# Four graph layers in one Trainium2 kernel: products and copies of the first layer and of the borders between layers reordered, and the third layer's bias rows written by ScalarE

## The chip, the core and the metric

The kernel runs on one core of one Trainium2 chip. The core has five engines with a program each: TensorE (PE in the rows, its weight loads PEld), VectorE (DVE), ScalarE (ACT), GpSimd (POOL) and SyncE (SP), which here only issues DMAs. The engines wait for each other by semaphores, and each works through its own list in the order in which it is written. The metric is the device time of one execution in microseconds (us); lower is better. The kernel before took 1655.96 us in the median of 3 runs (1653.0 to 1656.04).

## What is computed

Four message-passing layers follow one another over a graph of 50000 nodes with 128 features and 12500 edges sorted by target. Each is added to its input and normalized over the features:

```python
x = _layernorm(x + _L0_gnn_ref(x, edge_index, edge_weight, edge_attr_64, L0_gnn_Wq, ...))
x = _layernorm(x + _L1_gnn_ref(x, src, dst, L1_gnn_W1, L1_gnn_b1, L1_gnn_W2, L1_gnn_b2))
x = _layernorm(x + _L2_gnn_ref(x, L2_gnn_weight, src, dst, edge_type_8))
x = _layernorm(x + _L3_gnn_ref(x, L3_gnn_W_e, L3_gnn_b_e, L3_gnn_W_n, L3_gnn_b_n, src, dst,
                               edge_type_3, node_type_3))
```

The first layer is attention over the edges of a target (softmax by segments, plus `bias`), the second takes the mean of the sources and two linear maps with biases, the third multiplies each source by one of 8 matrices and sums, the fourth has 3 edge types and 3 node types: for a node of type t the result is `agg @ W_n[t].T + b_n[t]`, where `agg` begins with `relu(node_feature)`.

## The kernel before

Most nodes are the target of no edge, so for them a layer is the same dense map on all rows. The kernel therefore computes two things side by side: a dense pass over all 50000 rows, in NC = 100 blocks of 500 rows (4 tiles of 125 partitions), and the exact rows of the edges, in EC = 25 chunks of 500 edges. The dense results are written first, and in the last layer the rows of nodes with edges are scattered over them.

A dense block d goes through three stations. Its first-layer rows (`y0`, then normalized to `x1`) are made in step d; LAG = 3 blocks later the second layer (`y1` to `x3`), and 3 blocks later again the fourth (`sel` to `res`). One set of four PSUM banks, `po`, serves all of this: in each bank 3 × 128 columns hold the fourth layer's results for the three node types, and the last 128 the second layer's product z. So one round of TensorE is: `turn_rt` (transpose `x3`, ScalarE copies it to `rt` with a relu), `turn_xt` (transpose `x1`, ScalarE copies it to `xt`), then `dense_products`: `biased_slots` writes the bias rows `b_n` into the 3 × 128 columns of all four banks by a bf16 product (`po<-ball,ones_bf`), `types` adds `rt` times `wnt` on top, and `z_products` writes `xt` times `wab`. VectorE's `read(d)` then takes z out (L796), picks among the three types (L799, L800) and forms `sel` (L802). It increments `s_read`, which frees the banks for the next round. `measure` and `variances` give the variances of the new rows, ScalarE takes ln and exp of them (`first_roots`, "seed" in the rows), and VectorE's `scales` makes `rst` and `nmr` (L778 to L781) and increments `s_ln`; after it ScalarE normalizes (`third_rows`, `first_rows`, `results_of`, all L1074).

The order is written out by hand on every engine, as a loop over chunks c with one or two dense blocks in each step:

- First layer (lines "layer0"): two blocks per step. TensorE's step c has `back0(c)`, block 2c, the second half with block 2c+1, and between them the scores of chunk c+2, which end with `turn_targets0` (transpose of the gathered targets), ScalarE's copy `dt` and `score_targets` (L1500). ScalarE's slopes (L1151), differences and exponentials and VectorE's scans turn them into weights.
- Second layer: one block per step.
- Third layer: one block per step. VectorE makes masks for 7 relations (`masks`, L969), TensorE multiplies them with 8 matrices (`relations2`, L1627), VectorE scans the result by segments (`run<-same,run,pb`), TensorE transposes the scan (`pa<-ident,run`, L1645), and `target_rows2` adds it.
- Fourth layer: no dense block is left but the last few at the border.

Between the layers stand a few steps with dense blocks alone (`only_dense`), while the edge rows of the layer that ended are stored to HBM and gathered again by GpSimd for the next. GpSimd's gathers of node types (`types2`, 100 of them, needed at the start of the fourth layer) fill its free time.

## Time and profile before

| what | value |
|---|---|
| median of 3 runs | 1655.96 us |
| the profiled execution | 1652.15 us, of which the span of the trace is 1650.4 us |
| mean granted TensorE clock | 0.929 |
| busy share of the span | PE 84%, DVE 86%, ACT 67%, POOL 75% |
| first layer | 0 to about 590 us |
| second layer | about 612 to 889 us |
| third layer | about 933 to 1247 us |
| fourth layer | from about 1290 us |

The shares of the whole span mix stages with different limits, so the stretches have to be read by themselves. In a row of a timeline the first number is the start in us, the second how long the group lasted, and the note in brackets is the idle time before it with what ended it. "Granted clock" is the share of TensorE's full clock: 1.00 is 2.4 GHz and 0.50 is 1.2 GHz.

### The profile page before, as it was taken

The page shows a single profiled execution, that of the slowest core. Times are in us where ns is not written, and L with a number is a line of the kernel's source. Part 1 is how long each engine was busy: PE and PEld are TensorE (multiplying, and loading weights), DVE is VectorE, ACT ScalarE, POOL GpSimd, SP SyncE. Part 2 cuts the span into 40 slices and gives each one's busy share as a digit, 9 for nine tenths or more (in the row PEclk, how much of TensorE's full clock was granted, in tenths as well). Part 3 has the DMA queues.
Part 4 walks back from the last instruction along what each step waited for, and adds up shares of the span by engine and source line. Part 5 has one row for each costly group of instructions (what it writes and reads, how often), then busy time and mean ns, then how long its engine had stood idle before and what let it go on. Part 6 is the DMA issues. An engine that isn't in the chain of part 4 may idle for free.

```text
span 1650.4 us, 22899 instructions
## 1 busy us (share of the span) xinstructions
PE 1388.8 (84%) x6078; PEld 890.6 (54%) x6078; DVE 1419.0 (86%) x3056; ACT 1110.9 (67%) x2769; POOL 1230.3 (75%) x910
## 2 busy tenths in 40 slices
PE   3788877788778868777776899999996899999995
PEld 2455554555545546666665555555553455555552
DVE  5899899999899879999998799999995677777773
ACT  1678788887788787888888577777774344444441
POOL 7888888877777857888874567777778488888873
PEclk9798888988889879999998999999998899999997
DMA  7344444434444256767675455556554344344320
GB/s 172 94 100 102 111 109 110 112 91 115 111 113 105 58 139 177 189 179 192 182 187 149 131 149 164 156 157 165 151 133 111 83 97 96 96 97 97 96 70 20
DMA packets 165797, 205.06 MB, mean 124 GB/s; under 512 B 66825, under 2 KB 97920, under 8 KB 165668
## 3 DMA queue, kind: packets, MB, share of 16 engines
q1 hardware_dynamic: 108068, 179.45, 40.0%
q0 software_dynamic: 57600, 24.15, 9.0%
q8 instruction: 50, 0.82, 0.2%
q14 instruction: 79, 0.65, 0.2%
HBM read 147.12 MB, written 70.80 MB: 132 GB/s over the span
## 4 chain that ended last, share of the span: by engine, by line
PE 44%; DVE 32%; ACT 12%; issue 10%; POOL 1%; DMA 1%; SPq 0%; DVEq 0%; POOLq 0%; ACTq 0%
PE po L1391 23%; DVE bst L756 8%; DVE masked L969 6%; PE pt L1380 5%; PE pc L1500 3%; PE po L1386 3%; ACT x L1074 3%; DVE run L831 2%; PE po L1451 2%; DVE y L796 2%; DVE po L799 2%; DVE sel L802 2%; DVE po L800 2%; ACT do L1074 2%; PE pa L1672 1%
## 5 line engine op out<-in xcount | busy, mean ns | idle before, releaser
L536 POOL DMA_INDIRECT xs<-target_rows,slot_all x236 | 322.2, 1365 | 140.9 <-issue 60.9
L1074 ACT ACTIVATE x<-y,nmr,rst 125x128 f32<-125x128 f32 x800 | 322.5, 483 | 29.6 <-issue 18.4
L1391 PE MATMUL po<-wnt,rt 128*125 128x384 f32 x800 | 297.4, 518 | 0.0
L1380 PE MATMUL pt<-ident,x 125*128 125x125 f32 x800 | 122.3, 276 | 110.5 <-issue 110.5
L1391 PEld LDWEIGHTS po<-wnt,rt 128*125 128x125 f32 x800 | 162.7, 206 | 96.9 <-issue 21.2
L1391 PE MATMUL po<-wnt,run 128*125 128x384 f32 x600 | 201.5, 486 | 0.0
L543 POOL DMA_INDIRECT out_rows<-do,last_all x100 | 146.5, 1465 | 63.0 <-issue 40.6
L1380 PEld LDWEIGHTS pt<-ident,x 125*128 125x128 f32 x800 | 93.1, 145 | 148.4 <-issue 147.1
L536 POOL DMA_INDIRECT xs<-in_x,src_all x100 | 143.2, 1432 | 34.7 <-issue 33.8
L1074 ACT ACTIVATE do<-yd,nmr,rst 125x128 f32<-125x128 f32 x400 | 163.5, 483 | 5.4 <-DVE nmr L781 4.6
L1074 ACT ACTIVATE res<-sel,nmr,rst 125x128 f32<-125x128 f32 x400 | 163.7, 484 | 2.6 <-DVE nmr L781 1.8
L1627 PE MATMUL pb<-masked,wr 128*128 128x500 f32 x350 | 156.5, 588 | 2.2 <-DVE masked L969 2.2
L536 POOL DMA_INDIRECT slot_all<-slot_d,src_all x100 | 131.9, 1319 | 30.5 <-issue 30.5
L536 POOL DMA_INDIRECT ntd_all<-in_ntype,dst_all x100 | 129.4, 1294 | 30.5 <-issue 30.5
L543 POOL DMA_INDIRECT slot_d<-eid,last_all x100 | 128.5, 1285 | 30.5 <-issue 30.2
L756 DVE BATCH_NORM_STATS2 bst<-y 125x6 f32<-125x256 f32 x400 | 143.1, 420 | 3.8
L1391 PEld LDWEIGHTS po<-wnt,run 128*125 128x125 f32 x600 | 108.9, 188 | 68.7 <-issue 0.6
L1140 ACT ACTIVATE st<-pt 128x500 f32<-128x500 f32 x50 | 29.3, 585 | 142.1 <-issue 95.1
L536 POOL DMA_INDIRECT xdb<-target_rows,slot_all x64 | 86.6, 1352 | 44.2 <-issue 29.3
L536 POOL DMA_INDIRECT xd<-in_x,dst_all x68 | 94.9, 1396 | 27.2 <-issue 19.2
L1386 PE MATMUL po<-ball,ones_bf 128*125 128x384 bf16 x412 | 102.2, 379 | 13.0 <-DVE sel L802 13.0
L1451 PEld LDWEIGHTS po<-wab,xt 128*125 128x125 f32 x800 | 101.5, 188 | 19.8
(190 smaller groups left out, 3035.1 us busy)
## 6 DMA issues: line engine op xcount, KB each, us to landing
xin<-in_x SPq DMA_DIRECT2D x100, 224.0 KB
out_rows<-res SPq DMA_DIRECT2D x100, 224.0 KB
source_rows<-so SPq DMA_DIRECT2D x75, 224.0 KB
target_rows<-do SPq DMA_DIRECT2D x75, 224.0 KB
xs<-source_rows SPq DMA_DIRECT2D x59, 224.0 KB
same<-same_d SPq DMA_DIRECT2D x50, 250.0 KB
rel<-in_etype SPq DMA_DIRECT2D x50, 250.0 KB
xd<-target_rows SPq DMA_DIRECT2D x46, 224.0 KB
```

Of the source, the lines that this page charges most:

```text
L536: return nc.gpsimd.indirect_dma_start(out=to, out_offset=None, in_=table, in_offset=bass.IndirectOffsetOnAxis(ap=index, axis=0), bounds_ch ...
L543: return nc.gpsimd.indirect_dma_start(out=table, out_offset=bass.IndirectOffsetOnAxis(ap=index, axis=0), in_=of, in_offset=None, bounds_ch ...
L756: last = V.bn_stats(to, y[:, j:j + 2, :].rearrange("p j d -> p d j"))
L796: last = V.scalar_tensor_tensor(out=y1[(d - LAG) % 4][:, :, :], in0=of_z, scalar=0.0, in1=x1[(d - LAG) % 4][:, :, :], op0=ALU.max, op1=ALU ...
L969: V.scalar_tensor_tensor(out=masked[:, r, :], in0=rel[b][:, :], scalar=float(r), in1=st[:, :], op0=ALU.is_equal, op1=ALU.mult).then_inc(q[ ...
L1074: last = A(to[:, j, :], y[:, j, :], ACT.Identity, scale=rst[s][:, k:k + 1], bias=nmr[s][:, k:k + 1])
L1380: last = nc.tensor.transpose(tile_of(to, j), rows_[:, j, :], ident[0:R, 0:R])
L1386: mm(po[0:R, j * 512:j * 512 + NT * D], ones_bf[:, 0:R], ball[:, :, :].rearrange("k s d -> k (s d)"), start=True, stop=False, skip_group_c ...
L1391: last = mm(po[0:R, j * 512:j * 512 + NT * D], left(j), wnt[:, k, :, :].rearrange("k t d -> k (t d)"), start=start, stop=stop, skip_group_ ...
L1451: last = mm(po[0:R, j * 512 + NT * D:(j + 1) * 512], xt[:, j, :], wab[:, 0, :], start=False, stop=True, skip_group_check=True)
L1500: mm(pc[:, 0:C], qs[:, :], dt[:, :], start=False, stop=True).then_inc(q["pA"], 1)
L1627: mm(pb[:, 0:C], wr[:, r, :], masked[:, r, :] if r else st[:, :], start=r == 0, stop=r == REL - 1).then_inc(q["pM"], 1)
```

## The change

In the third layer, ScalarE writes a whole row `bfull` (the three bias rows and 128 zeros) into each of the four banks `po` by one ACTIVATE of 125 × 2048, `biased_slots2`. TensorE's bf16 product is gone there, and its `types` waits for `fB` in place of `s_read`. In the first layer TensorE multiplies block 2c+1's `types` ahead of the transposed targets and the scores, and ScalarE takes the roots ahead of the copy `dt`. At the borders, some copies, roots and gathers are put in another place, and 15 of GpSimd's type gathers move from the third layer into the last five steps of the second.

```diff
+        bfull = sb("bfull", [R, NT + 1, D])
...
 (GpSimd, second layer)
+                if SOONER * T + 3 * c >= EC * T:
+                    types2(typed, typed + 3)
+                    typed += 3
             types2(typed, typed + 2 * T)
...
 (VectorE, set-up)
+            V.memset(bfull[:, NT, :], 0.0)
+            V.tensor_copy(bfull[:, 0:NT, :], brow[0:R, :, :])
...
 (ScalarE, first layer)
             for c in range(EC):
                 s = chain_of(2 * c) % 2
                 first_roots(s, 8)
+                if c >= 1 and there(c + 1):
+                    evacuate_targets(c + 1, 0, 0, dt, ACT.Copy)
                 if there(c + 1):
                     slopes0(c + 1)
...
                     target_rows0(c, TAIL, 0)
+                    evacuate_rt(2 * EC - 2)
                     source_rows0(c, s)
+                    evacuate_xt(2 * EC - 2)
+                    first_roots(chain_of(2 * EC) % 2, 4)
                     results_of(2 * c, s, 2)
                     results_of(2 * c + 1, s, 3)
-                if there(c + 2):
-                    evacuate_targets(c + 2, 0, 0, dt, ACT.Copy)
-            only_dense(2 * EC)
+            chain_rows(2 * EC)
...
 (ScalarE, third layer)
+            def biased_slots2(c):
+
+                act.wait_ge(s_read, block_of(2, c) + 1)
+                A(po[0:R, :].rearrange("p (j k) -> p j k", j=T), bfull[:, :, :].rearrange("p s d -> p (s d)").unsqueeze(1).broadcast_to([R, T, 512]),
+                  ACT.Copy).then_inc(ph[2]["fB"], 1)
...
                 act.wait_ge(s_ln, k + 1)
                 third_rows(d, k % 2, 0)
+                biased_slots2(c)
                 evacuate_rt(d - 1)
                 first_rows(d, k % 2, 2)
...
 (ScalarE, start of the fourth layer)
             targets3(0)
+            evacuate_sources(1, 3, 0)
             dense_chain(NC + 2 * LAG - 1)
-            evacuate_sources(1, 3, 0)
...
 (TensorE, first layer)
                     turn_xt(2 * c + 1)
+                    if 2 * c + 1 >= LAG:
+                        type_products(2 * c + 1)
+                    else:
+                        pe.wait_ge(s_read, 2 * c + 4)
+                        biased_slots()
                     if there(c + 2):
                         turn_targets0(c + 2)
+                    z_products(2 * c + 1).then_inc(s_z, 1)
+                    if there(c + 2):
                         score_targets(c + 2)
-                    dense_products(2 * c + 1)
...
 (TensorE, start of the third layer)
             dense_turns(d - 2)
-            dense_products(d - 2)
             pe.wait_ge(ph[1]["rd"], EC)
             turns2(0)
+            dense_products(d - 2)
...
 (TensorE, third layer)
                 if there(c + 1):
                     relations2(c + 1, range(REL // 2, REL))
-                dense_products(d - 2)
+                    pe.wait_ge(q["fB"], c + 1)
+                    pe.wait_ge(s_rt, d - 4)
+                    last = types(lambda j: rt[:, j, :], 0, stop=False)
+                    if d - 2 < NC:
+                        last = z_products(d - 2)
+                    last.then_inc(s_z, 1)
+                else:
+                    dense_products(d - 2)
```

The semaphore `s_fill` is also folded into `s_const`, whose waits count one higher.

On ScalarE one step of the third layer runs from the roots (`seed`) to the next roots. `x_1<-y_1` are the third rows, `rt` and `xt` the copies of the two transposes, `st` the copy of the sources. Before:

```order
L1083 ACTIVATE seed<-seed 125x16 [waits s_logs]
L1074 ACTIVATE x_1<-y_1,nmr,rst 125x128 [waits s_ln]
L1074 ACTIVATE x_1<-y_1,nmr,rst 125x128 x3
L1111 ACTIVATE rt<-pt 128x500 [waits s_tr]
L1074 ACTIVATE x_0<-y_0,nmr,rst 125x128 x4
```

Now:

```order
L1089 ACTIVATE seed<-seed 125x16 [waits s_logs]
L1080 ACTIVATE x_1<-y_1,nmr,rst 125x128 [waits s_ln]
L1080 ACTIVATE x_1<-y_1,nmr,rst 125x128 x3
L1288 ACTIVATE po<-bfull 125x2048 [waits s_read]
L1117 ACTIVATE rt<-pt 128x500 [waits s_tr]
L1080 ACTIVATE x_0<-y_0,nmr,rst 125x128 x4
```

The fill of the four banks stands behind the rows that wait for `s_ln`, and ahead of the copy `rt`.

On TensorE the end of one step of the third layer and the start of the next, from the last relations. Before:

```order
L1627 MATMUL pb<-masked,wr 128x500 [waits layer2_vM] x3
L1386 MATMUL po<-ball,ones_bf 125x384 [waits s_read]
L1386 MATMUL po<-ball,ones_bf 125x384 x3
L1391 MATMUL po<-wnt,rt 125x384 [waits s_rt]
L1391 MATMUL po<-wnt,rt 125x384 x3
L1451 MATMUL po<-wab,xt 125x128 [waits s_xt]
L1451 MATMUL po<-wab,xt 125x128 x3
L1645 MATMUL pa<-ident,run 125x128 [waits s_ln,layer2_vA]
L1645 MATMUL pa<-ident,run 125x128 x3
L1380 MATMUL pt<-ident,x_0 128x125 [waits s_xt,s_x3]
```

Now:

```order
L1653 MATMUL pb<-masked,wr 128x500 [waits layer2_vM] x3
L1411 MATMUL po<-wnt,rt 125x384 [waits s_rt,layer2_fB]
L1411 MATMUL po<-wnt,rt 125x384 x3
L1471 MATMUL po<-wab,xt 125x128 [waits s_xt]
L1471 MATMUL po<-wab,xt 125x128 x3
L1671 MATMUL pa<-ident,run 125x128 [waits s_ln,layer2_vA]
L1671 MATMUL pa<-ident,run 125x128 x3
L1400 MATMUL pt<-ident,x_3 128x125 [waits s_xt,s_x3]
```

The bias product is gone; the product with `rt` waits for `fB`, and everything of the next step stands behind it.

On TensorE the second half of a step of the first layer, from the transpose of `x1` of block 2c+1 to the first row of the next step (`xdb` are the gathered targets). Before:

```order
L1380 MATMUL pt<-ident,x_3 128x125 [waits s_xt,s_rt,s_x1]
L1380 MATMUL pt<-ident,x_3 128x125 x3
L1380 MATMUL pt<-ident,xdb 128x125 [waits s_xt,layer0_eS,layer0_gd_2]
L1380 MATMUL pt<-ident,xdb 128x125 x3
L1500 MATMUL pc<-dt,qs 128x500 [waits layer0_eD]
L1386 MATMUL po<-ball,ones_bf 125x384 [waits s_read]
L1386 MATMUL po<-ball,ones_bf 125x384 x3
L1391 MATMUL po<-wnt,rt 125x384 [waits s_rt]
L1391 MATMUL po<-wnt,rt 125x384 x3
L1451 MATMUL po<-wab,xt 125x128 [waits s_xt]
L1451 MATMUL po<-wab,xt 125x128 x3
L1514 MATMUL pb<-ident,run 125x128 [waits layer0_vL,layer0_nF,layer0_vA]
```

Now:

```order
L1400 MATMUL pt<-ident,x_3 128x125 [waits s_xt,s_rt,s_x1]
L1400 MATMUL pt<-ident,x_3 128x125 x3
L1406 MATMUL po<-ball,ones_bf 125x384 [waits s_read]
L1406 MATMUL po<-ball,ones_bf 125x384 x3
L1411 MATMUL po<-wnt,rt 125x384 [waits s_rt]
L1411 MATMUL po<-wnt,rt 125x384 x3
L1400 MATMUL pt<-ident,xdb 128x125 [waits s_xt,layer0_eS,layer0_gd_2]
L1400 MATMUL pt<-ident,xdb 128x125 x3
L1471 MATMUL po<-wab,xt 125x128 [waits s_xt]
L1471 MATMUL po<-wab,xt 125x128 x3
L1520 MATMUL pc<-dt,qs 128x500 [waits layer0_eD]
L1534 MATMUL pb<-ident,run 125x128 [waits layer0_vL,layer0_nF,layer0_vA]
```

The score product moved from ahead of the block's products to behind them.

## Rows read from the trace of the kernel before

**Rows 1.** Busy time by stage: stretch, its length, each engine's busy time, clock, DMA.

```profile
0.00:590.00 590.00, 460.53 (x2028) 296.87 (x2028) 516.32 (x1085) 440.80 (x1112) 469.29 (x350) 0.86 0.46 109
933.00:1247.00 314.00, 306.67 (x1242) 183.82 (x1240) 304.58 (x663) 228.44 (x587) 226.22 (x170) 1.00 0.57 151
```

**Rows 2.** VectorE's scans by layer: duration min/median/max ns, first and last start.

```profile
L831 DVE TENSOR_TENSOR_SCAN run<-masked,run,aux x25: 1259/1260/1262, 31.0 to 564.2; 128x500 f32<-128x500 f32 x25
L831 DVE TENSOR_TENSOR_SCAN run<-same,run,pb x25: 1244/1257/1257, 933.3 to 1246.2; 128x500 f32<-128x500 f32 x25
```

**Rows 3.** Timeline of one step of the third layer.

```profile
1013.19 0.70 PE L1645 MATMUL pa<-ident,run 128*125 128x128 f32 x4 [0.31 <-DVE run L831]
...
1014.36 0.59 ACT L1111 ACTIVATE rt<-pt 128x500 f32<-128x500 f32 x1 [0.73 <-issue]
...
1016.58 0.68 DVE L796 SCALAR_TENSOR_TENSOR y<-po,x 125x512 f32<-125x512 f32 x1
...
1018.63 0.69 DVE L802 SCALAR_TENSOR_TENSOR sel<-x,po 125x512 f32<-125x512 f32 x1
...
1021.73 0.81 PE L1386 MATMUL po<-ball,ones_bf 128*125 128x384 bf16 x4
...
1022.38 2.74 PE L1391 MATMUL po<-wnt,rt 128*125 128x384 f32 x8
...
1024.01 0.22 ACT L1083 ACTIVATE seed<-seed 125x16 f32<-125x16 f32 x1
...
1024.88 0.18 DVE L781 SCALAR_TENSOR_TENSOR nmr<-bst,rst 125x16 f32<-125x16 f32 x1
...
1024.96 1.04 PE L1451 MATMUL po<-wab,xt 128*125 128x128 f32 x8
...
1025.10 1.65 ACT L1074 ACTIVATE x<-y,nmr,rst 125x128 f32<-125x128 f32 x4 [0.87 <-DVE nmr L781]
...
1026.31 0.70 PE L1645 MATMUL pa<-ident,run 128*125 128x128 f32 x4 [0.31 <-DVE run L831]
```

**Rows 4.** ScalarE's copies without pointer operands: count, busy us, mean ns.

```profile
L1140 ACT ACTIVATE st<-pt 128x500 f32<-128x500 f32 x50 | 29.3, 585 | 142.1 <-issue 95.1 <-PE pt L1380 47.1
...
L1169 ACT ACTIVATE den<-pc 125x12 f32<-125x12 f32 x25 | 4.5, 180 | 37.3 <-PE pa L1518 31.8 <-issue 5.5
```

**Rows 5.** TensorE by microsecond at the third layer's end: busy, granted clock, DMA.

```profile
1251.00:1252.00 1.00, 0.00 (x0) 1.00 0.62 125
...
1253.00:1254.00 1.00, 0.00 (x1) 0.50 0.05 1
...
1259.00:1260.00 1.00, 1.00 (x6) 0.99 0.76 96
```

**Rows 6.** Timeline of the same stretch, TensorE.

```profile
1254.00 1.54 PE L1386 MATMUL po<-ball,ones_bf 128*125 128x384 bf16 x4 [5.38 <-DVE sel L802]
1255.33 4.57 PE L1391 MATMUL po<-wnt,rt 128*125 128x384 f32 x8
```

**Rows 7.** Timeline of one step of the first layer, its second half.

```profile
233.69 0.62 PE L1380 MATMUL pt<-ident,x 125*128 125x125 f32 x4 [2.06 <-issue]
...
237.49 2.04 PE L1500 MATMUL pc<-dt,qs 128*128 128x500 f32 x2 [0.68 <-ACT dt L1145]
...
237.84 0.19 DVE L778 SCALAR_TENSOR_TENSOR tmp<-seed 125x32 f32<-125x32 f32 x1 [1.08 <-ACT seed L1083]
...
239.56 0.59 ACT L1151 ACTIVATE masked<-pc 128x500 f32<-128x500 f32 x1 [1.75 <-PE pc L1500]
```

**Rows 8.** Timelines at the three borders.

```profile
599.40 1.06 PE L1380 MATMUL pt<-ident,x 125*128 125x125 f32 x4 [11.45 <-issue]
...
919.75 0.17 DVE L778 SCALAR_TENSOR_TENSOR tmp<-seed 125x16 f32<-125x16 f32 x1 [8.70 <-ACT seed L1083]
...
1262.04 1.27 POOL L536 DMA_INDIRECT xdb<-target_rows,slot_all  x1 [0.30 <-issue]
...
1285.89 2.03 PE L1672 MATMUL pa<-st,wet 128*128 128x500 f32 x2 [7.40 <-ACT st L1140]
```

More of the change, by code:

```diff
@@ L158, in gnn_kernel @@
             sem, ("s_w0", "s_w1", "s_w2", "s_w3", "s_same", "s_idx", "s_slotrow", "s_prep", "s_scr", "s_pe0", "s_bp", "s_const"))
[L159 to L160 removed]
+        s_rdeg, s_rd, s_hs, s_last, s_turned, s_carry, s_before = map(
+            sem, ("s_rdeg", "s_rd", "s_hs", "s_last", "s_turned", "s_carry", "s_before"))
         s_xin, s_res = [sem(f"s_xin{i}") for i in range(4)], two(sem, "s_res")
@@ L277, in _ @@
             sp.dma_start(nt_all[:, :, :], ntypeP).then_inc(s_last, 16)
-            sp.wait_ge(s_fill, 1)
+            sp.wait_ge(s_const, 2)
             sp.dma_start(slot_d.rearrange("(p t) o -> p (t o)", p=R), fill[:, :]).then_inc(s_slotrow, 16)
@@ L527, in _ @@
             nc.gpsimd.memset(prv[:, :], -1).then_inc(s_const, 1)
-            nc.gpsimd.memset(fill[:, :], SKIP).then_inc(s_fill, 1)
+            nc.gpsimd.memset(fill[:, :], SKIP).then_inc(s_const, 1)
             nc.gpsimd.iota(row_id[:, :], pattern=[[1, PM]], base=0, channel_multiplier=PM)
@@ L570, in types2 @@
                     gather(ntd_all[:, i // T, i % T:i % T + 1], ntype3, dst_all[:, i // T, i % T:i % T + 1], N - 1).then_inc(s_types, 16)
-            pool.wait_ge(s_const, 2)
+            pool.wait_ge(s_const, 3)
             pool.wait_ge(s_idx, 80)
@@ L684, in _ @@
             step = chain.step
-            dve.wait_ge(s_const, 2)
+            dve.wait_ge(s_const, 3)
             dve.wait_ge(s_idx, 80)
@@ L1124, in dense_chain, with chain_rows @@
             def dense_chain(d):
+                first_roots(chain_of(d) % 2, 4)
+                chain_rows(d)
+            def chain_rows(d):
                 k = chain_of(d)
-                first_roots(k % 2, 4)
                 act.wait_ge(s_ln, k + 1)
@@ L1415, in setup_carry @@
                 mm(pb[0:1, D:D + R], rdeg_p[:, PM - 1:PM], ident[0:R, 0:R], start=True, stop=True).then_inc(s_carry, 1)
-                pe.wait_ge(s_const, 2)
+                pe.wait_ge(s_const, 3)
                 pe.wait_ge(s_turned, 2)
```

4 lines of the change are left out of this document (1 added, 3 removed).

## The prediction

> **What bounds the kernel now.** I read the busy times by stage first, then the periods of each loop, then the timeline of one step of each stage that the change touches, and the borders last. In the third layer two engines are full: VectorE is busy 304.58 us of 314 and TensorE 306.67, at the full clock (2.4 GHz), while ScalarE has 228.44 [rows 1]. Its 25 scans start from 933.3 to 1246.2 [rows 2], and in the step shown the period is 1026.31 - 1013.19 = 13.12 us [rows 3]. VectorE sets it: L796 and `sel` have no wait noted, and TensorE's only idle time in the step is the 0.31 us before `pa<-ident,run`, which waits for VectorE's scan. L796 starts at 1016.58, though the z products before it, the twins of those at 1024.96, had been done for over 3 us. So TensorE's bias product, 1022.38 - 1021.73 = 0.65 us a step, hides behind VectorE, and removing it alone would give nothing there.
>
> In the first layer no engine is full (VectorE 516.32 us of 590, TensorE 460.53, ScalarE 440.80) and the clock is 0.86 [rows 1]. The loop takes (564.2 - 31.0)/24 = 22.2 us a step on average [rows 2] and goes round by handoffs: copy of a transpose, next transpose, copy `dt`, score, slopes [rows 7].
>
> **Third layer: where the fill lands.** In step c TensorE's `types` wants ScalarE's fill number c+1. By the order on ScalarE that fill stands behind the third rows, which wait for `s_ln` of the same step c. Take the step of [rows 3]. VectorE frees the banks when `sel` ends, at 1019.3; TensorE reaches `types` at 1021.73. But the last of VectorE's scales (L781) starts at 1024.88, and the third rows, which wait for it, at 1025.10. They take 1.65 us, so the fill starts at 1026.75. The banks have been free for 7.4 us by then, and TensorE has stood for 5. The wait for `s_read` costs nothing; it is the place behind `s_ln` that costs.
>
> Behind the waiting `types` on TensorE are the z products, the transposes of the scan, and `turn_rt`. VectorE's L796 waits for z, and ScalarE's copy `rt`, which stands right behind the fill, waits for `turn_rt`. So the fill closes a ring that was open before, in which each link waits for the one ahead:
>
> - fill on ScalarE. No row shows ScalarE writing PSUM. From 180 ns at 12 columns and 585 ns at 500 [rows 4] a column costs 0.83 ns, and 2048 columns make 180 + 2036 × 0.83 = 1870 ns. Below, 1.2 us, if a write to PSUM were a third cheaper than one to SBUF; above 3.7 us, if it were twice as dear. I take 1.87, as the rows are copies of the same kind. (The Trainium skill's page "ScalarE: Activation LUTs", section "Step-by-step: what each stage is for", calls PSUM the quicker port of the two for a ScalarE result; no run here shows it, and by it the fill would be nearer the lower end.)
> - weights, `types` and z on TensorE. From 1022.38 to 1024.96 and 1.04 more is 3.62 us; with the first weight load (some 0.15) and the handoff (0.05) 3.82 us at full clock.
> - from the first `pa<-ident,run` to the third rows of the next step: 1025.10 - 1013.19 = 11.91 us [rows 3]. ScalarE has its whole list here (`rt`, first rows, `st`, `xt`, source rows, target rows, results, roots), and it waits for TensorE at `rt` already in the row (0.73 us), so the stretch begins with that handoff and can't shrink much.
> - third rows: 1.65 us.
>
> Sum: 1.87 + 3.82 + 11.91 + 1.65 = 19.25 us a step, against 13.12.
>
> The clock comes on top. TensorE works some 12.5 us in such a step (13.12 less its wait of 0.31 and the bias product), so it is idle for 6.7 us in each. In [rows 6] it has been idle for 5.38 us before 1254.00; in [rows 5] the granted clock is 1.00 at 1251, 0.50 (1.2 GHz) at 1253 and back at 1259. The eight products there start at 1255.33, behind the bias product at 1254.00, and last 4.57 us against 2.74 at full clock [rows 3], 1.83 more. Without a bias product ahead of them they meet the slow stretch from its start, and at half clock throughout they would take 2.58 us more. I take 2.1. That makes 21.35 us a step, 8.2 more than before.
>
> The Trainium skill has a rule on this: its page "TensorE: Matmul & The Clock Gate", section "HAM oscillation — how this bites in real kernels", says that a loop with a long enough idle stretch in every round is throttled in every round again, so that the cost is paid each time. The trace agrees at this one place, with its 0.50 at 1253 [rows 5]; without the rule's repetition the sum stays at 19.25 us a step.
>
> 24 steps (c = 0 to 23) have a fill. 24 × 8.2 = 197, less 2 for the first one, where only VectorE's leg is late: **+195 us**.
>
> **First layer.** TensorE now does the bias product and `types` of block 2c+1 (0.65 + 2.58 at full clock) between the transpose that ends at 234.31 and the turning of the targets, which is on the path to the score. The transposes are then done at 238.1 (0.6), `dt` at 238.8 (0.6, as the copies of [rows 4]) and the score, half of 2.04 at full clock, at 240.2, the z products standing before it. ScalarE's slopes start at 240.3 and not at 239.56 [rows 7]: 0.7 us later. In return, at the step's start TensorE has no products of block 2c+1 left to do, and ScalarE no longer waits at `den`: that wait is 31.8 us in 25 steps, 1.3 each [rows 4]. Taking the roots first removes VectorE's 1.08 us at L778 [rows 7]; but its next wait is then for the slopes, so this only moves. Net 0.6 a step in 24 steps, **-15 us**. Bounds: if VectorE's 1.08 counted as well, -40; if `types`, now on the path, ran at half clock, 2.6 us a step more, +45.
>
> **Borders.** First to second: TensorE's 11.45 us without work before 599.40 [rows 8] shrink, as the copies `rt` and `xt` and the roots go ahead of the results (8 activations, 3.2 us): -3, no more, since the second layer also needs its first gathers. Second to third: VectorE's 8.70 us at 919.75 end 5 us earlier, because `turns2(0)` no longer waits for a block's products; GpSimd's 15 type gathers come before its first gathers of the third layer and delay them a little, into that gap: -5. Third to fourth: the first gathers of the fourth layer, at 1262.04, stood behind 17 type gathers, of which 2 are left, and start when the last target rows have landed, some 3 us sooner; `st` of chunk 1 is copied before the last dense chain, which cuts the 7.40 us before 1285.89 by some 2 on the path: -5. Together **-13**, with bounds from 0 to -22.
>
> Filling `bfull` is a copy of 384 columns and a small memset on VectorE at the start, and the changed count of `s_const` orders nothing anew: 0, or 1 us if no wait covers them.
>
> **Sum.** 1652.15 + 195 - 15 - 13 = **1819 us**. The profiled execution lies 0.2% below the median of the runs, so this may come out some 4 us higher.
>
> **The rivals.**
> 1. The ring closes, but the clock stays up: 24 × 6.13 - 2 - 28 = +117, **1769 us**. Transposes and relations fill 12.5 us of each step; against it stands [rows 5].
> 2. Only VectorE's leg of the ring is closed. If ScalarE found slack in its list, the step would be third rows 1.65, fill 1.87, products 3.82 and then VectorE from L796 to the end of its scales, 1025.06 - 1016.58 = 8.48: 15.8 us, with the clock's 2.1 17.9. 24 × 4.8 - 28 = +87, **1739 us**. Against it: ScalarE's list is in order, and its 9.5 us of work a step (228.44/24) start only behind `rt`.
> 3. The other side: the fill is hidden. If ScalarE could write the banks in the gap from 1019.3 to 1021.7, TensorE would never wait, VectorE would go on setting 13.12 us, and only the 28 us of reorderings would be left: **1624 us**. It decides at whether the fill of step c is ahead of TensorE's `types` of step c; the order puts it 5 us behind.
> 4. The clock falls in the first layer too, with `types` on the path: 24 × 2.6 = +62, **1881 us**. Before, it fell there after two gaps close together; now the 2.06 us before 233.69 [rows 7] are followed by unbroken work.
>
> **How the numbers follow.** Forecast (ring with clock) 0.68, rival 1 0.15, rival 2 0.07, rival 3 0.04, rival 4 0.06. The range runs from just below rival 1, 1758, to a fill twice as dear, 1819 + 24 × 1.85 = 1863. A measurement of this kernel can tell some 0.2% from no change. Faster has rival 3 and a little more, 0.05; nothing lands within 0.2% but by chance, 0.01; slower 0.94.
>
> **What would show it.** In the profile after: `po<-wnt,rt` in the third layer has a wait of 6 to 7 us ended by ScalarE's `po<-bfull`, 24 times; the scans there are 21 us apart (19 if the clock holds); VectorE waits for z ahead of `y<-po,x` and for the seeds ahead of its scales; the fill lasts 1.9 us; the granted clock of the stretch is 0.8 to 0.85; the fourth layer is as long as before. In the first layer `den` waits less, the slopes' wait is longer and the one before L778 is gone. The prediction is wrong if the scans of the third layer stay 13.1 us apart.

## The result and the profile after

| | median | range | ratio to the kernel before (95%) |
|---|---|---|---|
| before | 1655.14 us | 1653.0 to 1656.04 | |
| changed | 1832.69 us | 1830.92 to 1835.58 | 1.1084 [1.1071, 1.1098] |

The changed kernel is 10.8% slower (four runs of each). Left out of all medians and ratios are three much longer executions, one of the last experiment's kernel (1948.29 us) and two of the repeated kernel before (1757.99 and 6931.33 us). The changed kernel's profiled execution took 1830.92 us with a span of 1829.1 us, 178.7 us more than the 1650.4 us of before. The mean granted clock fell from 0.929 to 0.890.

I divided the span at VectorE's scans, which both kernels have in the same number. They start so in the changed kernel (line, engine, operation, count, shortest/median/longest ns, first and last start in us):

```profile
L837 DVE TENSOR_TENSOR_SCAN run<-masked,run x50: 1247/1256/1261, 38.5 to 605.7; 128x500 f32<-128x500 f32 x50
L837 DVE TENSOR_TENSOR_SCAN run<-same,run,st x25: 1251/1255/1262, 633.1 to 909.5; 128x500 f32<-128x500 f32 x25
L837 DVE TENSOR_TENSOR_SCAN run<-same,run,pb x25: 1250/1256/1258, 953.5 to 1433.6; 128x500 f32<-128x500 f32 x25
```

| stretch, between scans | before | changed | difference |
|---|---|---|---|
| to the first layer's last scan | 584.7 | 605.7 | +21.0 |
| border to the second layer | 28.1 | 27.4 | -0.7 |
| second layer | 274.5 | 276.4 | +1.9 |
| border to the third layer | 46.0 | 44.0 | -2.0 |
| third layer | 312.9 | 480.1 | **+167.2** |
| border to the fourth layer | 31.7 | 30.7 | -1.0 |
| first two steps of the fourth layer | 28.8 | 21.1 | -7.7 |
| the rest of it | 302.5 | 302.5 | 0 |

From the last scan to the end both kernels take about 41.2 us, and the differences add up to the 178.7 us. The third layer has nearly all of it. The +1.9 us of the second layer lie in its first interval alone (12.37 us where it was 10.45), so the first border and what follows from it cost 1.2 us and give nothing. Busy time by stage, in the columns of [rows 1]:

```profile
0.00:611.00 611.00, 457.39 (x2028) 297.62 (x2028) 515.60 (x1086) 442.30 (x1111) 465.65 (x350) 0.85 0.44 105
953.00:1434.00 481.00, 326.92 (x1139) 184.67 (x1137) 309.03 (x664) 269.12 (x610) 222.33 (x165) 0.84 0.37 98
```

VectorE has the same work there as before (309.03 us against 304.58) but 481 us to do it in, and TensorE's clock fell from 1.00 to 0.84. No engine is full any more: this is a stage that waits. The waits of the third layer say for whom (engine, tile and line, the one waited for, then us in all, times, longest):

```profile
PE po L1411 <- ACT po L1288: 153.4, 23, 6.7
ACT rt L1117 <- PE pt L1400: 145.4, 23, 6.3
DVE y L802 <- PE po L1471: 98.0, 23, 4.8
DVE masked L975 <- PE pb L1653: 45.4, 22, 2.7
```

TensorE waits for ScalarE's fill, ScalarE for a transpose of TensorE, VectorE for TensorE's z: each waits for another once a step. One turn of this, where before stood [rows 3]:

```profile
1212.18 0.17 DVE L787 SCALAR_TENSOR_TENSOR nmr<-bst,rst 125x16 f32<-125x16 f32 x1
...
1212.39 1.65 ACT L1080 ACTIVATE x<-y,nmr,rst 125x128 f32<-125x128 f32 x4 [0.91 <-DVE nmr L787]
...
1213.95 1.86 ACT L1288 ACTIVATE po<-bfull 125x2048 f32<-125x2048 f32 x1
...
1215.86 4.47 PE L1411 MATMUL po<-wnt,rt 128*125 128x384 f32 x8 [6.70 <-ACT po L1288]
...
1220.16 1.04 PE L1471 MATMUL po<-wab,xt 128*125 128x128 f32 x8
...
1221.04 0.60 PE L1671 MATMUL pa<-ident,run 128*125 128x128 f32 x4
1221.24 0.69 DVE L802 SCALAR_TENSOR_TENSOR y<-po,x 125x512 f32<-125x512 f32 x1 [4.16 <-PE po L1471]
...
1222.10 0.59 ACT L1117 ACTIVATE rt<-pt 128x500 f32<-128x500 f32 x1 [6.30 <-PE pt L1400]
...
1232.85 1.65 ACT L1080 ACTIVATE x<-y,nmr,rst 125x128 f32<-125x128 f32 x4 [0.88 <-DVE nmr L787]
```

From one third rows to the next are 1232.85 - 1212.39 = 20.46 us; between the sixth scan of the layer and the twenty-first the mean is 20.48. The granted clock in this turn (TensorE by microsecond, as [rows 5]):

```profile
1211.00:1212.00 1.00, 0.00 (x0) 1.00 0.87 254
1213.00:1214.00 1.00, 0.00 (x0) 0.50 0.79 205
1218.00:1219.00 1.00, 1.00 (x3) 0.50 0.62 125
1220.00:1221.00 1.00, 1.00 (x10) 1.00 0.12 2
```

It falls to 1.2 GHz while TensorE stands idle in front of the fill, is low through most of `types`, and is back at 2.4 GHz for z.

In the first layer, one step with the slow stretch behind the score (compare [rows 7]):

```profile
243.32 0.56 ACT L1117 ACTIVATE rt<-pt 128x500 f32<-128x500 f32 x1
...
250.08 0.59 ACT L1161 ACTIVATE masked<-pc 128x500 f32<-128x500 f32 x1 [1.20 <-PE pc L1520]
...
251.58 0.67 PE L1534 MATMUL pb<-ident,run 128*125 128x128 f32 x4 [1.54 <-DVE masked L848]
...
255.18 0.16 ACT L1179 ACTIVATE den<-pc 125x12 f32<-125x12 f32 x1
...
255.54 2.00 PE L1526 MATMUL pa<-st,wv 128*128 128x500 f32 x2 [1.86 <-ACT den L1180]
...
258.17 1.88 PE L1509 MATMUL pc<-ea,es 65*128 65x500 f32 x2
...
260.56 0.59 ACT L1150 ACTIVATE st<-pt 128x500 f32<-128x500 f32 x1 [0.55 <-PE pt L1400]
```

Ahead of the score the step is now as planned (it takes 1.07 us and not 2.04). But TensorE has nothing to do behind it, 1.54 and then 1.86 us, since the block that used to stand there now stands ahead. The same places before:

```profile
233.02 0.57 ACT L1111 ACTIVATE rt<-pt 128x500 f32<-128x500 f32 x1
...
246.08 0.18 ACT L1169 ACTIVATE den<-pc 125x12 f32<-125x12 f32 x1 [1.32 <-PE pa L1518]
...
246.47 1.08 PE L1506 MATMUL pa<-st,wv 128*128 128x500 f32 x2
...
247.81 1.01 PE L1489 MATMUL pc<-ea,es 65*128 65x500 f32 x2
...
249.55 0.58 ACT L1140 ACTIVATE st<-pt 128x500 f32<-128x500 f32 x1
```

The granted clock in the changed kernel is 0.50 from 254 to 260:

```profile
252.00:253.00 1.00, 1.00 (x12) 1.00 0.29 65
254.00:255.00 1.00, 0.00 (x0) 0.50 0.14 10
259.00:260.00 1.00, 1.00 (x3) 0.50 0.64 163
```

At the borders, the gathers of the fourth layer start 1450.29 - 1433.6 = 16.7 us behind the last scan, where it was 15.9 us, and the wait for `st` of 7.40 us [rows 8] is 0.68:

```profile
1450.29 1.27 POOL L537 DMA_INDIRECT xdb<-target_rows,slot_all  x1 [45.25 <-DMA target_rows<-do]
...
1465.57 1.11 PE L1705 MATMUL pa<-st,wet 128*128 128x500 f32 x2 [0.68 <-ACT st L1150]
```

### The profile page after: what moved, and what is told of

Its sections match the earlier page's. It is cut to its first block, busy times and chain, and to the rows that moved or that the text cites. A ratio compares the mean times of both kernels' runs of the same rounds, so it can differ in the third digit from the quotient of the medians.

```text
span 1829.1 us, 22757 instructions
## 1 busy us (share of the span) xinstructions
PE 1406.3 (77%) x5982; PEld 894.0 (49%) x5982; DVE 1423.2 (78%) x3058; ACT 1154.7 (63%) x2793; POOL 1230.3 (67%) x910
## 4 chain that ended last, share of the span: by engine, by line
PE 54%; ACT 20%; DVE 17%; issue 7%; POOL 1%; DMA 1%; SPq 0%; ACTq 0%; POOLq 0%; DVEq 0%
PE po L1411 27%; ACT x L1080 6%; PE pt L1400 6%; DVE bst L762 5%; PE pb L1653 4%; ACT res L1080 4%; PE po L1471 3%; PE pa L1526 3%; ACT po L1288 2%; ACT do L1080 2%; PE po L1406 2%; DVE run L837 2%; PE pc L1509 2%; ACT so L1295 2%; PE pc L1520 1%
## 5 line engine op out<-in xcount | busy, mean ns | idle before, releaser
L537 POOL DMA_INDIRECT xs<-target_rows,slot_all x236 | 326.8, 1385 | 263.5 <-DMA xs<-source_rows 180.4
L1411 PE MATMUL po<-wnt,rt 128*125 128x384 f32 x800 | 325.2, 557 | 156.6 <-ACT po L1288 156.6
L1080 ACT ACTIVATE x<-y,nmr,rst 125x128 f32<-125x128 f32 x800 | 322.3, 481 | 28.8 <-DVE nmr L787 28.8
L1411 PEld LDWEIGHTS po<-wnt,rt 128*125 128x125 f32 x800 | 170.6, 219 | 284.2 <-ACT po L1288 176.0
L1400 PE MATMUL pt<-ident,x 125*128 125x125 f32 x800 | 137.4, 300 | 105.3 <-issue 105.3
L1400 PEld LDWEIGHTS pt<-ident,x 125*128 125x128 f32 x800 | 103.4, 157 | 156.7 <-issue 156.6
L802 DVE SCALAR_TENSOR_TENSOR y<-po,x 125x512 f32<-125x512 f32 x100 | 68.7, 687 | 138.1 <-PE po L1471 138.1
L544 POOL DMA_INDIRECT slot_d<-eid,last_all x100 | 137.6, 1376 | 30.5 <-issue 30.5
L537 POOL DMA_INDIRECT xs<-in_x,src_all x100 | 133.5, 1335 | 34.9 <-issue 34.6
L1117 ACT ACTIVATE rt<-pt 128x500 f32<-128x500 f32 x100 | 57.3, 573 | 156.1 <-PE pt L1400 156.1
L975 DVE SCALAR_TENSOR_TENSOR masked<-rel,st 128x500 f32<-128x500 int32 x175 | 107.0, 671 | 45.4 <-PE pb L1653 45.4
```

What stands on the lines that cost most here:

```text
L537: return nc.gpsimd.indirect_dma_start(out=to, out_offset=None, in_=table, in_offset=bass.IndirectOffsetOnAxis(ap=index, axis=0), bounds_ch ...
L544: return nc.gpsimd.indirect_dma_start(out=table, out_offset=bass.IndirectOffsetOnAxis(ap=index, axis=0), in_=of, in_offset=None, bounds_ch ...
L802: last = V.scalar_tensor_tensor(out=y1[(d - LAG) % 4][:, :, :], in0=of_z, scalar=0.0, in1=x1[(d - LAG) % 4][:, :, :], op0=ALU.max, op1=ALU ...
L975: V.scalar_tensor_tensor(out=masked[:, r, :], in0=rel[b][:, :], scalar=float(r), in1=st[:, :], op0=ALU.is_equal, op1=ALU.mult).then_inc(q[ ...
L1080: last = A(to[:, j, :], y[:, j, :], ACT.Identity, scale=rst[s][:, k:k + 1], bias=nmr[s][:, k:k + 1])
L1117: A(rt[:, :, :], by_tile(pt), ACT.Relu).then_inc(s_rt, 1)
```

## The experiments

All ratios are to the kernel before, run on the same chip in the same session. "Step" is the mean distance of the third layer's scans 6 to 21, or in the first layer that of its scans `run<-masked,run,aux` from the sixth on. My theory was: the third layer's ring costs some 165 us, the first layer costs 21 where a gain was forecast, the borders give a little.

### The parts by themselves

**The third layer undone.** The changed kernel with the third layer as before:

```diff
                 third_rows(d, k % 2, 0)
-                biased_slots2(c)
                 evacuate_rt(d - 1)
...
-                    pe.wait_ge(q["fB"], c + 1)
-                    pe.wait_ge(s_rt, d - 4)
-                    last = types(lambda j: rt[:, j, :], 0, stop=False)
...
+                dense_products(d - 2)
```

> The changed kernel with the third layer as it was before (TensorE writes the bias rows by its product, no fill on ScalarE). If the stages add up as the two traces show them (third layer +167 us, first layer +21, the rest -9.5), this takes 1655 + 21 - 9.5 = 1667 us. Rival: the reorderings are a gain of 28 us as forecast, and the loss in the first layer only comes with the rest: 1627 us.

Measured: 1657.99 us, 1.0027 [1.0017, 1.0038]. The third layer is back at 312.9 us, the first one stays at 606.9, and the border to the fourth is 24.6 us where the changed kernel has 30.7. So the ring also hides some 6 us of what the edits at that border give. All the other edits together are a small loss and not the gain of 28 us that I forecast. The edits at the borders were not run by themselves.

**The third layer alone.** The kernel before, with nothing but the fill, its order and its wait:

```diff
                 third_rows(d, k % 2, 0)
+                biased_slots2(c)
...
+                    pe.wait_ge(q["fB"], c + 1)
+                    pe.wait_ge(s_rt, d - 4)
+                    last = types(lambda j: rt[:, j, :], 0, stop=False)
```

> The kernel before with the third layer's part of the change alone. Ring theory: its scans are 20.5 us apart, and it takes 1655 + 167 = 1822 us. Rival: part of the loss came from the gathers moved by GpSimd or from the start of the third layer, so that it is under 1800.

Measured: 1820.49 us, 1.1004 [1.0982, 1.1026], steps of 20.49 us, third layer 482.3 us. This part accounts for nearly all of the 10.8%.

**TensorE's order of the first layer alone.** The kernel before, with the block 2c+1 moved:

```diff
+                    if 2 * c + 1 >= LAG:
+                        type_products(2 * c + 1)
...
                     if there(c + 2):
                         turn_targets0(c + 2)
+                    z_products(2 * c + 1).then_inc(s_z, 1)
+                    if there(c + 2):
                         score_targets(c + 2)
-                    dense_products(2 * c + 1)
```

> The kernel before with TensorE's new order in the first layer alone (bias product, types, targets, z, score). If this order causes the first layer's loss by moving the slow stretch of TensorE's clock onto values0 and the transposes, it takes the +21 us and more, since the roots still stand behind the copy of the targets: 1676 to 1690 us. Rival (ScalarE's order causes the loss): 1655 or less.

Measured: 1680.32 us, 1.0166 [1.0148, 1.0184]; the last scan of the layer starts at 610.7 us, 26.0 later than before. The loss in the first layer comes from this order. The steps are 23.89 us, and 23.87 in the changed kernel; the 5 us that this kernel loses beyond the changed one's 21.0 lie in the first five steps.

**Roots first alone.** ScalarE takes the roots ahead of the copy `dt`, and nothing else is changed:

```diff
                 first_roots(s, 8)
+                if c >= 1 and there(c + 1):
+                    evacuate_targets(c + 1, 0, 0, dt, ACT.Copy)
...
-                if there(c + 2):
-                    evacuate_targets(c + 2, 0, 0, dt, ACT.Copy)
```

> The kernel before with ScalarE's new order in the first layer alone (roots ahead of the copy of the targets). VectorE's wait of 1.08 us for the seeds goes; if that was on the path it gains up to 25 us (1630), if it only moves to the next wait it is the same, 1655. Rival: ScalarE is later at the copy by 0.5 us a step, 1667.

Measured: 1652.33 us, 0.9996 [0.9987, 1.0006], steps of 23.03 us as before. VectorE's wait for the seed only moved: from 100 to 550 us it waited 17.3 us there before and 11.6 for z; now it waits 10.8 us behind the slopes (L841) and 17.1 for z.

### Is it the fill's place, its length, or the clock?

**The fill in the gap.** The fill of step c+1 is issued in step c behind `xt` and ahead of the source rows, where the banks have just been read; the work is the same.

```diff
+            biased_slots2(0)
             for c in range(EC - 1):
...
                 third_rows(d, k % 2, 0)
-                biased_slots2(c)
...
                 evacuate_xt(d - 1)
                 if there(c + 2):
+                    biased_slots2(c + 1)
                     source_rows2(c + 2)
```

> The changed kernel, with ScalarE's fill of step c+1 put ahead of the source rows of step c, where VectorE has just freed the banks; the same 24 fills, no wait for the scales in front of them. Ring theory: TensorE no longer waits 6.7 us for it and the clock stays up; but ScalarE's list had no slack ahead of the roots (they start the moment the results end), so 1.9 us of work there lengthens the step to 14.9: 1667 + 24 x 1.8 = 1710 us. Rival (VectorE sets the pace and a fill is hidden anywhere off the ring): 13.1 us a step, 1667 us. Rival (the fill itself, its write into PSUM, is what costs): 20 us a step, 1830.

Measured: 1729.38 us, 1.0459 [1.0441, 1.0478], steps of 16.22 us, not the 14.9 that I expected. More than half of the loss is gone with the place alone. What is left shows in one step (timeline):

```profile
1152.12 1.89 ACT L1288 ACTIVATE po<-bfull 125x2048 f32<-125x2048 f32 x1
...
1154.69 2.74 PE L1412 MATMUL po<-wnt,rt 128*125 128x384 f32 x8
...
1159.02 0.17 DVE L784 SCALAR_TENSOR_TENSOR tmp<-seed 125x16 f32<-125x16 f32 x1 [2.76 <-ACT seed L1089]
...
1161.06 0.70 PE L1672 MATMUL pa<-ident,run 128*125 128x128 f32 x4 [2.75 <-DVE run L837]
```

TensorE doesn't wait for the fill any more, and `types` runs at full clock. But the fill has pushed ScalarE's roots back. VectorE waits 2.76 us for them, its scan is late, TensorE idles 2.75 us for the scan, and the clock falls at the relations that follow:

```profile
1161.00:1162.00 1.00, 0.94 (x8) 1.00 0.78 238
...
1163.00:1164.00 1.00, 1.00 (x2) 0.50 0.73 228
```

The clock is also most of the miss. From the second step on to the last but two, the layer's steps take either 15.1 to 15.2 us, near the 14.9, or 16.6 to 16.7. In all short ones the granted clock is 1.00 throughout, in all long ones its mean is 0.90.

**The fill in the gap and the roots first.** The same, with the results' rows (`results_of`) moved behind the roots of the next step, so that the roots don't wait for the added 1.9 us:

```diff
                 first_roots(k % 2, 4)
+                if c >= 1:
+                    results_of(d - 1, (k - 1) % 2, 1)
...
-                if there(c + 2):
-                    results_of(d, k % 2, 1)
```

> As the kernel with the fill in the gap, but ScalarE takes the roots ahead of the results, so that 1.5 us of rows leave the path to the roots and 1.9 us of fill are on it. Theory (ScalarE's list ahead of the roots sets the step there): 13.5 us a step instead of 16.2, and with so little idle time on TensorE the clock stays at 1.00; 1729 - 24 x 2.7 = 1664 us, at best equal to the third layer as it was before (1658). Rival (the fill itself slows TensorE or VectorE by their sharing of the banks): 15 us a step or more, 1700.

Measured: 1672.4 us, 1.0121 [1.0098, 1.0144], steps of 13.59 us against 13.12, third layer 324.6 us. VectorE's wait for the seed is down to 0.42 us:

```profile
1159.63 0.17 DVE L784 SCALAR_TENSOR_TENSOR tmp<-seed 125x16 f32<-125x16 f32 x1 [0.42 <-ACT seed L1089]
```

The same 24 fills, well placed, cost 11.7 us in the layer and not 167. They gain nothing either, since the bias product that they replace was hidden behind VectorE. The granted clock of the layer is 1.00 here, where it was 0.93 with the roots late.

**A small write in the fill's place.** ScalarE writes one column to a tile of its own where the fill stood, and TensorE makes its bias product itself, ahead of the same wait. What is left is the wait for a place in ScalarE's list:

```diff
+        tick = sb("tick", [R, 1])
...
-                A(po[0:R, :].rearrange("p (j k) -> p j k", j=T), bfull[:, :, :].rearrange("p s d -> p (s d)").unsqueeze(1).broadcast_to([R, T, 512]),
-                  ACT.Copy).then_inc(ph[2]["fB"], 1)
+                A(tick[:, :], none[:, :], ACT.Copy).then_inc(ph[2]["fB"], 1)
...
+                    pe.wait_ge(s_read, d + 1)
+                    for _ in range(1):
+                        biased_slots()
                     pe.wait_ge(q["fB"], c + 1)
```

> The changed kernel with ScalarE's fill replaced by a write of one column to another tile, at the same place in its list and with the same waits; TensorE makes the bias product itself, ahead of its wait for ScalarE. What is left is the wait alone. Ring theory: 1.7 us less in each round than the changed kernel, 20.47 - 1.7 = 18.8 us a step, 1833 - 24 x 1.7 = 1792 us. Rival (the length of the fill is the cost): 13.1 us a step, 1667 us.

Measured: 1801.39 us, 1.0888 [1.0864, 1.0912], steps of 19.41 us. Taking out the fill's 1.86 us of ScalarE's time saves only 1.07 a step, 24 us in the layer of the 167 (480.1 to 456.5). The miss of 0.6 us against the expected step is the clock's: `types` meets more of the slow stretch than in the changed kernel. From its start to the first `pa` are 5.85 us on average over 23 steps, against 5.20 there. It differs from step to step (4.2 to 5.5 us); one of the dear ones:

```profile
1162.77 5.48 PE L1411 MATMUL po<-wnt,rt 128*125 128x384 f32 x8 [4.35 <-issue]
```

**The same, with TensorE kept at work.** The bias product is made nine times over ahead of the wait, eight of them to no use:

```diff
                     pe.wait_ge(s_read, d + 1)
-                    for _ in range(1):
+                    for _ in range(9):
                         biased_slots()
                     pe.wait_ge(q["fB"], c + 1)
```

> As the kernel with the small write, but TensorE makes its bias product 9 times over before the wait (the last one counts), so that it is at work through most of the stretch in which it would stand idle. Ring theory with the clock: the products after the wait run at full clock and the step loses another 1.7 us, 17.1 us a step, some 40 us less than the kernel with the small write (1750 us). Rival (the clock has no part in it, the extra work is only in the way): the same as with the small write or more.

Measured: 1768.29 us, 1.0699 [1.0676, 1.0722], steps of 17.74 us.

```profile
1159.39 6.01 PE L1406 MATMUL po<-ball,ones_bf 128*125 128x384 bf16 x36
...
1164.33 0.19 ACT L1289 ACTIVATE tick<-none 125x1 f32<-125x1 f32 x1
...
1165.24 2.74 PE L1411 MATMUL po<-wnt,rt 128*125 128x384 f32 x8
```

The nine held `types` back until 1165.24, 0.7 us behind the write's end at 1164.52, so this is what the step has over the expected 17.1. The granted clock of the layer is 1.00, and `types` takes 2.74 us in every step. The same wait with TensorE at work costs 1.67 us a step less than with it idle (19.41 - 17.74). From the start of `types` to the first `pa` it is 2.4 us less (3.45 against 5.85), of which the nine take 0.7 back: the 2.4 are the clock's share.

### The first layer: the clock

**Useless products at two places.** The third layer undone (as in the first experiment), and in the first layer from its third step on, four further f32 products of 384 columns a step into the bank of the next transposes, two ahead of `back0` (the transposes of the scan and the products for the denominators) and two behind it; they are overwritten by what comes next:

```diff
+            def keep():
+                mm(pt[:, 0:NT * D], wnt[:, 0, 0, :], wnt[:, 0, :, :].rearrange("k t d -> k (t d)"), start=True, stop=True)
...
+                if c >= 2:
+                    for _ in range(2):
+                        keep()
                 back0(c)
+                if c >= 2 and c < EC - 1:
+                    for _ in range(2):
+                        keep()
```

> The changed kernel with the third layer as before, and two products without use (384 columns, fp32, into the free bank of the transposes) ahead of and two behind back0 in each step of the first layer from the third on, in the gaps after which the clock falls. Theory: the clock stays at 1.00 over values0, the transposes and the features, and the step goes from 23.9 to 22.0 us: 1667 - 22 x 1.9 = 1625 us. Rival (the clock is not the cause of the first layer's loss, or the extra products delay what stands behind them): 1667 us or more.

Measured: 1645.85 us, 0.9963 [0.9948, 0.9978]: a gain of 0.6% on the kernel without them (0.9963 against 1.0027), and not the 2% that I expected. From the fifth step on three take 21.9 us and all others 23.6. In the slow ones another gap, that for the turn of `xt`, lets the clock fall:

```profile
260.85 0.62 PE L1399 MATMUL pt<-ident,x 125*128 125x125 f32 x4 [2.07 <-issue]
...
262.32 2.13 PE L1410 MATMUL po<-wnt,rt 128*125 128x384 f32 x3
```

**At all gaps.** Three more ahead of that transpose, behind a wait for the bank's last reader (`keep` now takes the bank and the count):

```diff
+                    if c >= 2:
+                        pe.wait_ge(ph[0]["nF"], c + 1)
+                        keep(pb, 3)
                     turn_xt(2 * c + 1)
```

> As the kernel with the products without use in the first layer, and three more of them ahead of the transpose of x1 of block 2c+1, into the bank pb, where TensorE still stood idle for 2.07 us. In the trace of that kernel the steps in which the clock stayed up took 21.9 us and the others 23.6. Theory: all steps take 21.9; 1646 - 18 x 1.7 = 1615 us. Rival (the 21.9 us had another cause): 1646 us or more.

Measured: 1617.96 us, 0.9794 [0.9777, 0.9811]. Every step from the fifth on takes 21.9 us, and the layer's last scan starts at 566.6, 40.3 us earlier than in the first experiment, by nothing but useless work.

**The old order, kept busy.** The kernel before with the changed borders alone, and five useless products a step round the transpose of block 2c+1, where the old order has its two gaps close together:

```diff
+                    if c >= 2:
+                        pe.wait_ge(ph[0]["nF"], c + 1)
+                        keep(pb, 3)
                     turn_xt(2 * c + 1)
+                    if c >= 2:
+                        keep(pb, 2)
```

> The kernel before with the changed borders and the first layer in its old order, with three products without use ahead of the transpose of x1 of block 2c+1 and two behind it. Theory (in the old order too, the clock's slow stretch is on the path, through the targets' transposes and the score, 1.5 us a step): 23.05 - 1.5 = 21.6 us a step, 1655 - 16 (borders) - 22 x 1.5 = 1606 us. Rival (in the old order the slow stretch cost nothing, which is why it was the faster one): 1639 us.

Measured: **1606.91 us, 0.9719 [0.9702, 0.9736]**, steps of 21.26 us, last scan at 547.3. This is the fastest kernel of the study, 2.8% under the one before and 12% under the changed one. Busy time from 100 to 550 us of it, of the kernel before, and of the changed one:

```profile
100.00:550.00 450.00, 415.22 (x1992) 274.69 (x1991) 436.62 (x905) 394.36 (x993) 366.24 (x275) 1.00 0.48 114
```
```profile
100.00:550.00 450.00, 370.65 (x1651) 238.93 (x1650) 408.90 (x839) 361.71 (x915) 361.19 (x262) 0.87 0.44 106
```
```profile
100.00:550.00 450.00, 348.95 (x1582) 226.46 (x1583) 395.53 (x816) 350.25 (x882) 341.22 (x251) 0.86 0.43 103
```

The granted clock is 1.00 over the whole stretch, and VectorE is busy for 97% of it, so that it has next to no slack left. Of the 45.6 us by which the span is shorter than before, 37.4 lie ahead of the first layer's last scan; the other 8.2 come behind it, where the changed borders are.

**The old order, the places of the new one.** To tell whether the new order costs anything at full clock, the seven products of "at all gaps" stand in the old order:

```diff
+                if c >= 2:
+                    keep(pt, 2)
                 back0(c)
+                if c >= 2 and c < EC - 1:
+                    keep(pt, 2)
...
                         keep(pb, 3)
                     turn_xt(2 * c + 1)
-                    if c >= 2:
-                        keep(pb, 2)
```

> The kernel before with the changed borders, with useless products in the first layer at the very places and in the very number of e10_first_busy_all_gaps (2 before and 2 behind the weighted sum's product of the step, 3 ahead of the transpose of block 2c+1), so that it differs from e10 in the first layer only by TensorE's order (and ScalarE's roots, which e7 priced at nothing). Theory (the new order itself costs something, since types of block 2c+1 now stands ahead of the score even at full clock, and e11's 21.26 us a step against e10's 21.9 is that): steps of 21.3 us, first layer's last scan at 547 to 550, some 1608 us. Rival (the useless products behind the weighted sum cost the 0.64 us, and the order nothing): steps of 21.9 us, last scan at 565, some 1622 us. Third outcome: with the old order these places don't cover its gaps, the granted clock falls again, and the steps are 22.5 us or more, over 1635 us.

(The last two lines are against the fastest kernel.) Measured: 1662.4 us, 1.0050 [1.0036, 1.0064]; steps of 24.06 us on average, slower than the 23.03 without any. It is the third outcome: the old order has a gap behind its transpose of block 2c+1 that these places leave open, and the clock, 1.00 at 244, is 0.50 at 246.

```profile
245.16 0.62 PE L1390 MATMUL pt<-ident,xd 125*128 125x125 f32 x4 [1.44 <-ACT xt L1120]
246.45 2.04 PE L1510 MATMUL pc<-dt,qs 128*128 128x500 f32 x2 [0.68 <-ACT dt L1152]
```

At this clock the useless products at the other places win nothing back. Whether the 0.64 us a step between 21.9 and 21.26 is the order's or that of two more products is not settled.

## Why the prediction was right

1819 us were forecast and 1832.69 measured, inside the range. In the third layer the mechanism was the forecast one; the first layer had the wrong sign, which the total hides in part.

**Third layer: right, somewhat over.** The ring, link by link, from [rows 3] and [rows 4] and as measured in the turn above:

| link | forecast, us | measured, us |
|---|---|---|
| fill | 1.87 | 1.91 (the fill itself 1.857 in the median of 24) |
| weights, `types`, z, at full clock | 3.82 | 3.46 |
| the clock | 2.1 | 1.72 |
| first `pa<-ident,run` to the third rows | 11.91 | 11.81 |
| third rows | 1.65 | 1.56 |
| sum | 21.35 | 20.46 |

The measured products are those of the row: `types` from 1215.86 to 1220.16 is 4.30 us where the twins at full clock take 2.58, and z takes 0.88 to the first `pa`. Two terms were too large. The products' term took 0.36 us too much: 0.16, as 3.62 is from the start of one group to the modelled end of the other, and the next group starts before that end, and 0.2 for a weight load and a handoff that don't come on top. The clock cost 1.72 and not 2.1. The "some 12.5 us" of TensorE's work a step are 12.16 by their own terms (13.12 - 0.31 - 0.65); no term of the sum rests on them. The layer came out 28 us under the forecast. In the 22 full steps (20.48 us on average) 0.87 us each are 19 of it; the first and the last interval, 13.0 and 16.6 us, make the rest.

That it is the place in ScalarE's list, and not the fill's length, is shown: with the place mended the step is 13.59 us, with the length gone and the place kept it is 19.41. That the clock adds to it is shown by the busy wait. Rival 1, the ring with the clock up, falls by the 0.50 inside each turn, and rival 2, a step of 17.9 us, by the 20.48. Rival 3 had the right condition for the fill to be hidden, but not its whole price: in the gap the fill is hidden from TensorE, and ScalarE's list still had no 1.9 us to spare ahead of the roots (16.22 us), until the results moved too. Of the Trainium skill's page "TensorE: Matmul & The Clock Gate" (section "HAM oscillation — how this bites in real kernels") the statement that a loop with such an idle stretch pays for it every round is what this trace shows: 24 waits for the fill, and a mean clock of 0.84 in the stage.

**First layer: the wrong sign, -15 forecast and +21.0 measured.** The step that failed is "Net 0.6 a step in 24 steps, -15 us". Its two terms were near: the slopes start 6.76 us behind the copy `rt` and not 6.54, +0.2 where I had +0.7; from there to `den` are 5.10 us and not 6.52, -1.4 where I had -1.3. What I left out lies behind `den`. Up to the copy `st` it takes 5.38 us where it took 3.47, +1.9, because `pa<-st,wv` (2.00 us against 1.08) and `pc<-ea,es` (1.88 against 1.01), with the transposes between them, run at half clock. I had written that the 2.06 us before 233.69 "are followed by unbroken work" and did not ask what TensorE has to do in the place from which the block was taken. By the moved block that place got two waits, 1.54 and 1.86 us. Before, the slow stretch covered the score, the bias product and the first part of `types` of block 2c+1, and of what stood behind them ScalarE waited at length only at `den` (1.3 us a step, a term that the sum had); now it covers products that stand ahead of the transposes for the copies `xt` and `st`, and ScalarE waits at both (1.53 and 0.55 us in this step). Rival 4 named the clock, but put it on `types`, which runs at full clock (2.74 us), and priced it at +62. One of the signs was wrong as well: the slopes' wait for the score was to grow, and fell from 43.1 us in 25 steps to 30.4.

It is shown that TensorE's order does it (+26.0 with nothing else changed) and that the clock carries it: with the gaps filled, the new order's last scan starts at 566.6, 18 us earlier than in the kernel before, near the -15 of the sum. But by the same means the old order reaches 547.3, so the order isn't shown to be worth anything.

**Roots first: right.** The wait only moved (0.9996).

**Borders: -13 forecast, -11.4 measured, or -9.5 with the second layer's +1.9.** The single terms were off: I had -3, -5 and -5, and they are -0.7, -2.0 and -8.7 (-1.0 at the third border and -7.7 in the two steps behind it). At the first border TensorE's gap did shrink, from 11.45 us [rows 8] to 6.84, but the stretch only by 0.7, and the next interval grew by 1.9. At the third, the earlier copy of `st` takes away nearly the whole wait of 7.40 us, where I had 2 us of it on the path. The gathers, which I had start 3 us sooner, start 0.8 us later; with the third layer undone they start 10.6 us behind the last scan, 5.3 sooner, and that border and the two steps give -14.8 (24.6 and 21.1 us for 31.7 and 28.8). So the ring ate that part.

**The sum** came out near by luck, because two errors cancelled: -27.8 in the third layer, +36.0 in the first, +3.5 at the borders and in the second layer. Together they are 11.7 us, the difference between the 178.7 measured and the 167 forecast.

## What to carry to other kernels

Before work is moved from a busy engine to a free one, look at the place that it gets in the second engine's ordered list and at what that place itself waits for. If what it waits for depends on what the first engine still has to do, a ring closes, and its length is the new step, however free both engines are.

When a block is moved on TensorE, price the gap that it leaves too: if the clock falls in it, the products behind the gap take up to twice as long (here 2.00 us for 1.08), and what counts is who waits for them. Where such gaps can't be closed with real work, useless products in them are worth trying, with a look at the clock after each; placed past the gaps that matter they only cost.

## What was not expected of the hardware

- Useless products raise the speed of the whole loop. In the new order the first layer's step went from 23.88 to 21.9 us with seven more 384-column f32 products in it, in the old one from 23.03 to 21.26 with five. The granted clock of the stretch went from 0.87 (before) to 1.00, and the score from 2.04 us to 1.07 and 1.11.
- Where they stood at other places of the same loop, the clock of the stretch was 0.95 and the step 24.06 us, longer than the 23.03 at a clock of 0.87. The mean clock alone doesn't tell the time: what runs in the slow stretch does.
- ScalarE wrote 125 × 2048 f32 into TensorE's banks in 1856 to 1860 ns in 24 instances, 0.7% from the 1870 ns to which the prediction drew the copies of 12 and 500 columns out (placed in the gap, it took 1882 to 1889 ns). Those copies read these banks and write SBUF, the fill the other way round, so this shows that the estimate holds, and not which of the two is the cheaper to write.
- `types`, behind a wait for ScalarE with TensorE idle, took 4.47 us after a gap of 6.70 us, and with the small write, after one of 4.35, 5.48 us in the step shown (4.2 to 5.5 in others, 4.46 to 4.51 in the changed kernel). The longer gap was not the dearer one: there the clock had been at 0.50 since 1213 at the latest when the products began at 1215.86, and was back before they ended; behind the shorter one it was at 0.50 from 1162, the products began at 1162.77, and all of them met it.
